# Eight experts' second layer: three of four chunks as products of high and low parts instead of two, one high part made by VectorE

## The reference

```
logits = x @ Wr + br;  route_w = softmax(logits);  keep the top 2 of 8 experts, renormalize -> routed
h = relu(x @ W1[e] + b1[e])            # 8 experts, 128 -> 512
expert_out = h @ W2[e] + b2[e]         # 512 -> 128
y = sum_e routed[e] * expert_out[e]    # every expert is computed for every token
```

## Time and profile before

| | us |
|---|---|
| median of 3 runs | 1443.66 (1442.17 to 1443.86) |
| profiled execution | 1447.76 |
| its span in the trace | 1445.9 |
| busy in the span: PE, DVE, ACT, POOL | 1387.2, 1095.7, 1098.6, 837.4 |
| mean granted TensorE clock, share of full | 0.979 |

### The profile page before, as it was taken

How to read it: one execution, slowest core, us unless ns; L and a number is a source line. 1 busy time by engine, 2 the same in 40 slices (tenths; PEclk the granted TensorE clock), 3 DMA queues, 4 the chain that set the end, 5 groups by cost and what they waited for, 6 DMA issues and landing times.

```text
span 1445.9 us, 17857 instructions
## 1 busy us (share of the span) xinstructions
PE 1387.2 (96%) x6328; PEld 729.9 (50%) x6328; DVE 1095.7 (76%) x2009; ACT 1098.6 (76%) x945; POOL 837.4 (58%) x657
## 2 busy tenths in 40 slices
PE   6999999999999999999999999899999999999964
PEld 3434444434434444444444443356777777777743
DVE  6797788888888888887887887535678677686674
ACT  2699889969978978979979979935677676676741
POOL 5477777778778678768868867311333333333320
PEclk9999999999999999999999999899999999999985
DMA  3000110010001101101101103333011011010100
GB/s 111 1 16 17 24 45 17 23 38 23 24 17 45 23 17 45 24 17 31 38 16 31 30 16 98 89 125 104 2 66 59 8 67 59 8 67 27 41 8 7
DMA packets 45703, 54.97 MB, mean 38 GB/s; under 512 B 13808, under 2 KB 32368, under 8 KB 44464
## 3 DMA queue, kind: packets, MB, share of 16 engines
q1 hardware_dynamic: 45616, 53.84, 12.4%
HBM read 48.97 MB, written 4.85 MB: 37 GB/s over the span
## 4 chain that ended last, share of the span: by engine, by line
PE 89%; DVE 7%; ACT 1%; POOL 1%; issue 1%; DVEq 0%; POOLq 0%
PE av L406 15%; PE sc L393 14%; PE pj L74 13%; PE z L74 12%; PE y L1143 8%; PE sc L388 6%; PE y L74 5%; PE pj L370 4%; PE pj L434 4%; PE pj L414 2%; DVE w L578 2%; PE tb L1072 1%; PE tb L1086 1%; POOL wsum L310 1%; PE tb L1099 1%
## 5 line engine op out<-in xcount | busy, mean ns | idle before, releaser
L578 DVE TENSOR_SCALAR w<-sc 128x1024 f32<-128x1024 f32 x256 | 301.4, 1219 | 72.3 <-PE sc L393 65.4
L661 ACT ACTIVATE w<-w 128x2048 f32<-128x2048 f32 x128 | 237.5, 1904 | 131.4 <-DVE w L578 131.0
L310 POOL TENSOR_TENSOR wsum<-wsum,w 128x512 f32<-128x512 f32 x248 | 317.7, 1281 | 19.5
L919 POOL TENSOR_TENSOR hr_l<-hr,hr_h 128x512 fp32r<-128x512 f32 x112 | 150.2, 1341 | 262.7 <-ACT hr L967 262.7
L393 PE MATMUL sc<-query,key 64*128 64x512 f32 x1024 | 242.5, 593 | 0.0
L665 ACT ACTIVATE w<-w 128x2048 f32<-128x2048 f32 x128 | 240.3, 1901 | 0.4
L669 ACT ACTIVATE w<-w 128x2048 f32<-128x2048 f32 x128 | 239.6, 1895 | 0.0
L406 PE MATMUL av<-w,vt 128*64 128x512 f32 x1024 | 234.7, 600 | 0.8 <-ACT w L669 0.8
L967 ACT ACTIVATE hr<-z,b 128x512 f32<-128x512 f32 x256 | 173.5, 684 | 70.7 <-PE z L74 70.7
L296 POOL TENSOR_TENSOR sqq<-query 128x512 f32<-128x512 f32 x64 | 66.5, 1040 | 201.4 <-DVE query L518 187.7
L307 POOL TENSOR_TENSOR wsum<-w 128x512 f32<-128x512 f32 x124 | 158.6, 1279 | 4.7 <-ACT w L669 4.7
(11 more groups left out here) (189 smaller groups left out, 2291.7 us busy)
## 6 DMA issues: line engine op xcount, KB each, us to landing
hT<-head_recips SPq DMA_DIRECT2D x64, 256.0 KB, 4.0
rb<-routing SPq DMA_DIRECT2D x8, 2048.0 KB, 7.1
w<-in_W SPq DMA_DIRECT2D x16, 256.0 KB, 5.0
xa<-in_X SPq DMA_DIRECT2D x8, 256.0 KB, 4.4
xc<-in_X SPq DMA_DIRECT2D x8, 256.0 KB, 2.8
x<-xc SPq DMA_DIRECT2D x8, 256.0 KB, 4.1
out<-prod SPq DMA_DIRECT2D x8, 256.0 KB, 2.3
x<-x SPq DMA_DIRECT2D x1, 1792.0 KB, 7.9
```

The source lines that it names most:

```text
L310: nc.gpsimd.tensor_tensor(wsum[:, u, :], wsum[:, u, :], w[:, j % 2, u, c, :], ALU.add).then_inc(s_added, 1)
L578: nc.vector.tensor_scalar(w[:, s, 2 * r:2 * r + 2, c, :], sc[:, i, :, :], 0.0, None, ALU.max).then_inc(s_d2, 1)
L661: nc.scalar.activation(w[:, j % 2, u, :, :], w[:, j % 2, u, :, :], ACT.Sqrt).then_inc(s_sqrt, 1)
```

## The change

Chunks in parts are now n % 4 = 1, 2 and 3 (from batch 1 on) instead of 1 and 3: in each of the batches 1 to 7, eight fp32 matmuls of `expert` become products of three. For the new ones (n % 4 = 2) the high part is made by VectorE from the bank z(n), after hr(n) is written, at the head of its step; TensorE's `hidden(n + 2)` waits for it as well as for hr(n). GpSimd makes 24 low parts in a batch instead of 16. The split W2 grows from two to three chunks for each expert, is made one step later (steps 25 to 32), and TensorE waits for it expert by expert. The scratch of `token_ranks` shrinks to two rows that are used again for each of the four groups, and each group now ends in a wait of VectorE for its own semaphore. The rings of parts have 5 places instead of 3.

```diff
-        w1 = sb("w1", [P, NE, FF])
+        with ExitStack() as until_split:
+            w1 = until_split.enter_context(nc.sbuf_tensor("w1", [P, NE, FF], F32))
+        w2_l = sb("w2_l", [P, NE * (NF - 1), D], F32R)
+        scr = sb("scr", [P, 2, T])
...
-        N_T = 13
+        N_T = 16
...
         def in_parts(n):
-            return n >= NU and n % 2 == 1
+            return n >= NU and n % NF > 0
+        def by_vector(n):
+            return in_parts(n) and n % NF == 2
+        def highs(n):
+            return (n - NU - 2) // NF + 1
...
-            for n in range(NU + 1, B * NU, 2):
-                m = n // 2
-                pool.wait_ge(S["hr"], n + 1)
-                nc.gpsimd.tensor_tensor(hrs[1][:, m % (HR // 2), :], hr[:, n % HR, :],
-                                        hrs[0][:, m % (HR // 2), :].bitcast(F32), ALU.subtract).then_inc(S["lo"], 1)
+            for n in range(NU, B * NU):
+                if in_parts(n):
+                    pool.wait_ge(S["hr"], n + 1)
+                    if by_vector(n):
+                        pool.wait_ge(S["hi"], highs(n))
+                    nc.gpsimd.tensor_tensor(hrs[1][:, part(n) % HP, :], hr[:, n % HR, :],
+                                            hrs[0][:, part(n) % HP, :].bitcast(F32), ALU.subtract).then_inc(S["lo"], 1)
...  # TensorE, hidden(n)
                     pe.wait_ge(S["hr"], n - 1)
+                    if by_vector(n - 2):
+                        pe.wait_ge(S["hi"], highs(n - 2))
...  # ScalarE, hidden(n)
-                if in_parts(n):
+                if in_parts(n) and not by_vector(n):
...  # VectorE
-                if c == NC - 1:
-                    lt(t, ins)
+                lt(t, ins)
+            def high_part(n):
+                dve.wait_ge(S["hr"], n + 1)
+                V.tensor_scalar(hrs[0][:, part(n) % HP, :], z[:, n % 2, :], b1[:, n % NU:n % NU + 1], 0.0,
+                                ALU.add, ALU.max).then_inc(S["hi"], 1)
...  # VectorE, head of step(b, k)
+                if n < B * NU and by_vector(n):
+                    high_part(n)
```

More of the change, by code:

```diff
@@ L797, in build_rest @@
         score = sb("score", [P, NC])
-        scr = w1[:, :, :].rearrange("p (i c) t -> p i c t", i=2)
         above = sb("above", [P, 2, NC])
         keep = sb("keep", [P, 2, NC])
-        w2s = [sb("w2_h", [P, NE * NF // 2, D], F32R), sb("w2_l", [P, NE * NF // 2, D], F32R)]
-        hrs = [sb("hr_h", [P, HR // 2, T], F32R), sb("hr_l", [P, HR // 2, T], F32R)]
+        w2s = [sb("w2_h", [P, NE * (NF - 1), D], F32R), w2_l]
+        HP = 5
+        hrs = [sb("hr_h", [P, HP, T], F32R), sb("hr_l", [P, HP, T], F32R)]
         gel, res = o1, prod
@@ L812, in build_rest @@
         fa = psum("fa", [P, T])
-        names = """w2s lo in_x in_b2 in_rest_x in_last_x in_front in_tail ones2 w1s chain_f chain_t
+        names = """w2s lo hi in_x in_b2 in_rest_x in_last_x in_front in_tail ones2 w1s chain_f chain_t
                  stats_f mv_f std_f rstd_f xn_f turn_f xT_f logits exp rw rwT_ps rwT rwd rb xs z hr y ye ya yT_ps
@@ L848, in in_parts, with part @@
         def in_parts(n):
-            return n >= NU and n % 2 == 1
+            return n >= NU and n % NF > 0
[3 more added lines that the diff above has]
+            return (n - NU - 2) // NF + 1
+        def part(n):
+            return n // NF * (NF - 1) + n % NF - 1
         nat = "p (c d) -> p c d"
@@ L961, in hidden @@
                 act.wait_ge(S["z"], n + 1)
-                if in_parts(n):
+                if in_parts(n) and not by_vector(n):
                     if n == NU + 1:
                         act.wait_ge(att["x1_out"], 16 * B)
-                    nc.scalar.activation(hrs[0][:, n // 2 % (HR // 2), :], z[:, n % 2, :], ACT.Relu,
+                    nc.scalar.activation(hrs[0][:, part(n) % HP, :], z[:, n % 2, :], ACT.Relu,
                                          bias=b1[:, n % NU:n % NU + 1])
@@ L1134, in expert @@
                     pe.wait_ge(S["rwT"], 1)
-                if n == NU + 1:
-                    pe.wait_ge(S["w2s"], NE * NF)
                 pe.wait_ge(S["hr"], n + 1)
                 if in_parts(n):
-                    pe.wait_ge(S["lo"], (n - NU) // 2 + 1)
-                    m = product(nc, y[:, g % 2, :], [w[:, k // 2, :] for w in w2s],
-                                [v[:, n // 2 % (HR // 2), :] for v in hrs], start=False, stop=(i == NF - 1))
+                    if b == 1 and i == 1:
+                        pe.wait_ge(S["w2s"], 2 * (NF - 1) * (k // NF + 1))
+                    pe.wait_ge(S["lo"], part(n) - part(NU + 1) + 1)
+                    m = product(nc, y[:, g % 2, :], [w[:, part(k), :] for w in w2s],
+                                [v[:, part(n) % HP, :] for v in hrs], start=False, stop=(i == NF - 1))
                 else:
@@ L1330, in token_ranks @@
                 dve.wait_ge(S["score_ps"], t + 1)
-                V.tensor_scalar(scr[:, 0, c, :], tb[:, 1, :], score[:, c:c + 1], None, ALU.is_gt, ALU.add, accum_out=above[:, 0, c:c + 1])
-                ins = V.scalar_tensor_tensor(scr[:, 1, c, :], tb[:, 1, :], score[:, c:c + 1],
+                V.tensor_scalar(scr[:, 0, :], tb[:, 1, :], score[:, c:c + 1], None, ALU.is_gt, ALU.add, accum_out=above[:, 0, c:c + 1])
+                ins = V.scalar_tensor_tensor(scr[:, 1, :], tb[:, 1, :], score[:, c:c + 1],
                                              ttri[:, (NC - 1 - c) * P:(2 * NC - 1 - c) * P], ALU.is_equal, ALU.mult,
                                              accum_out=above[:, 1, c:c + 1])
-                if c == NC - 1:
-                    lt(t, ins)
+                lt(t, ins)
             def kept(t):
@@ L1362, in split_w2 @@
             def split_w2(e):
[L1363 to L1368, removed]
+                parts = slice((NF - 1) * e, (NF - 1) * (e + 1))
+                source = w2[:, NF * e + 1:NF * (e + 1), :]
+                V.tensor_copy(w2s[0][:, parts, :], source).then_inc(S["w2s"], NF - 1)
+                dve.wait_ge(S["w2s"], (NF - 1) * (2 * e + 1))
+                V.tensor_tensor(w2s[1][:, parts, :], source, w2s[0][:, parts, :].bitcast(F32),
+                                ALU.subtract).then_inc(S["w2s"], NF - 1)
+            def high_part(n):
+                dve.wait_ge(S["hr"], n + 1)
+                V.tensor_scalar(hrs[0][:, part(n) % HP, :], z[:, n % 2, :], b1[:, n % NU:n % NU + 1], 0.0,
+                                ALU.add, ALU.max).then_inc(S["hi"], 1)
             def weigh(g):
@@ L1454, in step @@
                     add_output(B - 1)
-                if b == 0 and k >= 24:
-                    if k == 24:
+                if 25 <= n < 25 + NE:
+                    if n == 25:
                         dve.wait_ge(att["x1_out"], 16 * B)
-                    dve.wait_ge(in_w2[k - 24], 16)
-                    split_w2(k - 24)
+                    dve.wait_ge(in_w2[n - 25], 16)
+                    split_w2(n - 25)
             att_step, weighted_values, sums, reciprocals, output, add_output = att_vector(dve)
```

## The result

The changed kernel takes 1487.55 us (median; 1485.04 to 1490.24) against 1443.63 for the kernel before: 3.03% slower, ratio 1.0303 with a 95% interval of 1.029 to 1.0316. That is +43.9 us where +24.0 was forecast; the direction was right, the time lies above the range of 1450 to 1484.

The account below looks back on a forecast made before the run. TensorE was taken to set the pace. Stalls net of TensorE's gain, +17.8 us, and one added GpSimd hold a batch, +6.2, made +24.0: median 1443.7 to 1467.7 us, range 1450 to 1484.

Parts of the forecast that it names:

- TensorE's gain: Each of 8 chunks in 7 batches becomes 0.17 us shorter: 1.36 us a batch, 9.5 in all.
- D: k = 22 (chunk 182): late high part delays yT and lg, then ScalarE's hr(183); z(185) stalls 1.2 us.
- E: k = 26 (chunk 186): den starts late behind lg, so the high part is late; z(188) stalls 0.95 us.
- A: k = 6 (chunk 166): the gelu keeps ScalarE, so hr and the high part are late; z(168) stalls 0.35 us.
- B: k = 10 (chunk 170): VectorE without idle time brings mv_t and the high part late; z(172) stalls 1.5 us.
- GpSimd's holds: Chunk 166's low part adds one hold of a VectorE pass, 1.03 us, falling on B in batches 2 to 7: +6.2.
- The second rival: Low parts hold VectorE three times a batch, before B, D and E: +12.4 us more, 1480; chance 0.18.
- At 2, 14, 18 and 30 ... I cost them at nothing.: Places where VectorE is free in time or TensorE has other matmuls: no cost; without cover up to 0.7 us each.
- C: Chunk 171: ScalarE waits for late mv_t, then loads a table, so hr(171) is late; z(173) stalls 0.5 us.
- the clock: Forecast is wrong if TensorE's clock falls below full in the new gaps; no size given.

## Why the prediction was wrong in size

**Right.** The cause and the sign: TensorE's gain of 0.17 us a chunk appears as such (k = 4, 16, 20, 24), the high part is late at k = 6, 10 and 26, and lg holds ScalarE at k = 22. D and E are as worked out, A nearly. Without extra holds the sum was B = 1.5; the kernel without the third low part has 1.37.

**The term that was mis-sized: GpSimd's holds.** I took one more between A and B, on the evidence of L1353 alone. There are two more, since the low parts of chunks 166 and 167 now run back to back, and each holds whatever VectorE turned to next in this stretch, passes of 128x4 numbers included. That is 1.1 us a batch in six batches. The second rival, three holds a batch on the way to B, D and E, had the right mechanism and 1480; its places were not right, since E needed no new one and D's took the place of an old one: the copy of `hand_over`, 1.5 us in both kernels. The prediction also equated a hold at each of the 8 low parts with this rival; eight holds would be 8.2 us a batch, not its 3.1.

**The step that failed: "At 2, 14, 18 and 30 ... I cost them at nothing."** At k = 30 the low parts of chunks 158 and 159 run back to back over the normalization of step 159:

```profile
1237.94 2.86 DVE L719 TENSOR_SCALAR xn_t<-x,mv_t,rstd_t 128x128 f32<-128x128 f32 x4
1240.84 0.69 DVE L1345 TENSOR_TENSOR prod<-xn_t,wrt 128x512 f32<-128x512 f32 x1
```

In the kernel before the four passes take 1.12 us. The score comes late, and TensorE loses 0.5 to 0.67 at k = 3. In the kernels without the third low part, with the high part by ScalarE, or without a change at k = 30 this is 0; with the high part by ScalarE the four passes take their old time in batch 5 (0.34 to 0.35 us each).

**The step that failed: C.** I put the table load behind the wait for mv_t, since in the row of before it starts at 1239.00, just at mv_t's end. That was chance: ScalarE had only then finished hr(170). After, the load runs at 1256.91 and the root comes 0.03 us behind mv_t. In the kernel without the third low part k = 13 changed by -0.10. C costs nothing, late as mv_t is.

**What stands in C's place: the clock.** Granted clock (the figure after the busy times) over the same 6 us of batches 3 to 7 in the changed kernel:

```profile
1132.00:1138.00 6.00, 5.51 (x15) 3.93 (x16) 4.22 (x7) 3.08 (x6) 3.06 (x3) 0.72 0.00 0
1196.00:1202.00 6.00, 5.04 (x13) 3.47 (x14) 4.70 (x10) 3.31 (x6) 2.94 (x3) 0.72 0.00 0
1261.00:1267.00 6.00, 5.41 (x15) 3.67 (x16) 4.33 (x7) 3.16 (x6) 3.48 (x3) 0.72 0.01 3
1325.00:1331.00 6.00, 4.77 (x19) 3.64 (x20) 5.09 (x14) 4.00 (x7) 3.62 (x3) 1.00 0.00 0
1388.00:1394.00 6.00, 4.80 (x12) 3.55 (x13) 4.89 (x13) 2.93 (x6) 2.51 (x2) 0.72 0.00 0
```

Behind the gap of 3.4 us at k = 12 TensorE falls to half clock (1.2 instead of 2.4 GHz). Batch 6 is the natural counterpart: same gap, full clock, and its change at k = 13 and 14 is -0.11 us, where batches 3 to 5 have +1.5. A mean of 0.72 over 6 us is 6 x 0.28 / 0.5 = 3.4 us at half. Taken against batch 6, the five drops cost 1.1 to 1.6 us each, 7.3 in all. In the kernel with k = 6 and 10 alone, all six batches have it (2.0 to 2.3 us where it is long, 1.1 to 1.3 where short). With gaps of 1.1 us or less at that place (no third low part, or the later low part) it is in none. Why batch 6 was spared I can't tell from one trace; and with the high part from hr the clock also fell behind two of the six waits of 1.8 us for the score, so the size of one gap alone doesn't decide it. The prediction named the clock as what would make it wrong, but gave it no price.

**The bill**, in us: forecast 24.0; the second new hold 6 x 1.04 = 6.2; the clock 7.3; C's term out, 6 x 0.63 = -3.8 (0.53 forecast, -0.1 found without the clock); k = 3, 3.6; the gain at k = 0 given back at k = 1, where ScalarE's hr is the tight wait, 6 x 0.2 = 1.2; A 6 x 0.16 = 1.0. Together 39.5, measured 41.0 in the stretch; 0.9 of the rest stands at k = 12 and 26 of batch 7. The remaining 3 us to 43.9 lie behind z(255), where 56.2 us became 58.2, and in the spread between executions.

The Trainium skill's rule in the prediction (SBUF — State Buffer, section "Who interferes with whom") has the trace on its side more fully than I gave it: the same section also counts `copy`, `cast` and `tensor_scalar` among the instructions that can contend, where their operands meet the conditions of a 2-port mode. Here `keep` and L719, both `tensor_scalar` from SBUF to SBUF, were held by 1.05 us and some 1.7 us (four passes, two low parts).

## What to carry to other kernels

An engine's spare time says little; take the longest unbroken run of work between two deadlines and count what is added to it, with every pass of another engine that can hold it. Where GpSimd gets more work, look for its passes coming back to back, and for the small VectorE passes under them. Where a wait on TensorE grows to 2 or 3 us, price the clock behind it (1.1 to 2.3 us a drop here); and convert only the places whose steps have slack: three of eight gave 0.2% here, where all eight cost 3%.

## What the hardware showed that I had not expected

- A VectorE pass over 128x4 numbers, 0.15 us by itself, takes 1.25 us under a low part of GpSimd of 1.3 to 1.4 us; the hold of 1.1 us is no shorter than that of a 128x128 pass (1.03).
- A hold can stay while the low part behind it changes: the copy of `hand_over` takes 1.50 us in both kernels, under different low parts, and 0.42 in the kernel with VectorE's high parts but no third low part.
- A table load of ScalarE runs ahead of the wait of the instruction that needs it, 3.9 us before that instruction.
